# Writing three bfloat16 parts to DRAM once and repeating them in the loads of the stacks

## The chip, the cores and the metric

The kernel runs on one core of one Trainium2 chip. The metric is the device time of one execution in microseconds (us). The kernel before took 806.59 us in the median of three runs (804.44, 806.59 and 806.61).

## The reference

Two transformer layers with a layer norm behind each half run on x of 4 batches, 512 tokens and 256 features. Layer 0 has an attention with 16 query heads and 4 key heads of 16 features (RMS norm, rotary embedding, no mask) and a mixture of eight experts beside a shared one. Layer 1 has a causal attention with 16 query and 16 key heads and a feed-forward layer whose weights come in 4 bits with a low-rank addition. What the change touches is the product of queries and keys in both attentions:

```
logits = jnp.einsum('btkgh,bskh->bkgts', q * scale, k)          # layer 0
scores = jnp.einsum('bnqd,bnkd->bnqk', q, k) * scale            # layer 1
x = _layernorm(x + _L0_attn_ref(x, ...)); x = _layernorm(x + _L0_ffn_ref(x, ...))
x = _layernorm(x + _L1_attn_ref(x, ...)); x = _layernorm(x + _L1_ffn_ref(x, ...))
```

## The kernel before

**Stacks.** Everything is float32, but the scores are computed in bfloat16 and must be nearly as exact. Each of q and k is therefore split into three bfloat16 parts (part 0 is the rounded value, part 1 the rounded rest, part 2 the rest of that), and six products of parts are summed by one matmul: for each head a stack of 6 x 16 = 96 rows is made, where q holds its parts in the order 0,0,0,1,1,2 and k in the order 0,1,2,0,1,0. A matmul over the 96 rows then gives q0k0 + q0k1 + q0k2 + q1k0 + q1k1 + q2k0. The stacks are `q_stack` and `k_stack` in layer 0, `cq_stack` and `ck_stack` in layer 1, each with two buffers for alternate batches.

**The way of the parts.** The projections come out with features on partitions, ordered (feature, head), so that a head's 16 features don't lie together. The parts (`parts`, `cparts`: partitions x 3 x 512 tokens) go to DRAM and come back in stack order. `layer0_parts` (issued at L532) and the `cK` steps of SP's last loop (L643) write each part as many times as the stack has it, in three transfers: 3, 2 and 1 copies (for k: parts 0 to 2, parts 0 and 1, part 0). One store is 64 partitions (k of layer 0) or 128 partitions by 1 KB rows. Then `layer0_stacks` (L544 for k, L548 and L549 for the first eight heads of q, L553 for the last eight) and `layer1_stacks` (L628) load them. In layer 1 a load is a head group (four heads): 96 rows of 4 KB, one for q and one for k; two groups make a half (128 features), and a batch has two halves.

**Order of the work.** SP issues every one of these transfers from one queue in program order. In layer 0 it issues, for each batch: wait for the parts of k, store; wait for the parts of the first half of q, store; wait for the store of k, load k; wait for the store of q, load q in two transfers; wait for the parts of the second half, store, wait for that, load. Between the batches SP issues the loads of the expert weights (`gate_up_load`, L558; three of 1 MB after each of the first two batches, one after the third). In layer 1 each half is stored as its parts come (`cparts_ready`), and after the k of a half SP waits for the stores (`cs_scr`) and issues four loads. The second half of batch 1 comes behind step `cM` instead, at which SP also moves the row maxima into two more stack rows (`m_t`, two transfers at L650, semaphore `s_m`).

TensorE works through the lists `A_*` and `C_*` in their written order, and never goes ahead of a step that waits. `attS` (matmuls at L744) waits for `s_stack`, `s_stack1` or `s_stack2` at the first use of a load. In layer 1 `max` (L904, which finds the row maxima) is the first to use a stack and waits for `cs_stack` once per head group; `cattS` (L928) recomputes the scores with the maxima and waits for `s_m` at the start of a batch. ScalarE waits for the stores before it overwrites a part (`T` at L995, `cQ` at L1108).

Of the kernel before, what the change touches and what calls it, by code (L numbers as in the profile page):

```python
# [22 lines left out]
BF16 = mybir.dt.bfloat16  # L23
# [7 lines left out]
B = 4  # L31
# [119 lines left out]
def post_ln_layers(nc, ins, out):  # L151
# [4 lines left out]
    with ExitStack() as ctx:  # L156
# [193 lines left out]
        def cparts_of(b, i):  # L350

            return cparts_first[:, i % 2] if b == 0 and i >= 2 else cparts[:, i % 2]

        qscr = nc.dram_tensor("q_stacks_dram", [B, 2, 6, P, S], BF16).ap()
        kscr = nc.dram_tensor("k_stack_dram", [B, 6, KV0 * HD, S], BF16).ap()
        cscr = nc.dram_tensor("stacks_dram", [B, 2, 2, 6, P, S], BF16).ap()
# [148 lines left out]
        def _(sp):  # L505
# [17 lines left out]

            def layer0_parts(b, i):

                w = qk_width(i)
                for j in range(3):
                    if i == 0:
                        dst, src = kscr[b], parts[0:w, 0, 0:3 - j, :]
                    else:  # L530
                        dst, src = qscr[b, i - 1], parts[0:w, i % 2, j:j + 1, :].to_broadcast([w, 3 - j, S])
                    sp.dma_start(dst[(0, 3, 5)[j]:(3, 5, 6)[j]].rearrange("r p n -> p r n"), src).then_inc(s_scr[i % 2], 16)  # L532

            def layer0_stacks(b):

                sp.wait_ge(parts_ready, 3 * b + 1)
                layer0_parts(b, 0)
                sp.wait_ge(parts_ready, 3 * b + 2)
                layer0_parts(b, 1)
                sp.wait_ge(s_scr[0], 96 * b + 48)  # L540
                if b >= 2:

                    sp.wait_ge(pv_done, head0 * (b - 1))
                sp.dma_start(k_stack[0:STACK, b % 2, :, :], kscr[b].rearrange("r (d h) n -> (r d) h n", d=HD))\  # L544
# [7 lines left out]
                sp.wait_ge(s_scr[0], 96 * (b + 1))  # L552
                sp.dma_start(q_stack[0:STACK, b % 2, NH // 2:NH, :], qscr[b, 1].rearrange("r (d h) n -> (r d) h n", d=HD))\  # L553
                  .then_inc(s_stack2[b % 2], 16)
# [64 lines left out]
            def layer1_stacks(b, half):  # L619
                if b >= 2 and half == 0:  # L620

                    sp.wait_ge(pv_done, head0 * B + headc * (b - 1))
                for t in range(2):
                    sp.wait_ge(cs_scr[t][half], 48 * (b + 1))
                for hg in (2 * half, 2 * half + 1):
                    for t, dst in ((0, cq_stack), (1, ck_stack)):
                        rows = cscr[b, t, half].rearrange("r (d h) n -> (r d) h n", d=HD)
                        sp.dma_start(dst[0:STACK, b % 2, 4 * hg:4 * (hg + 1), :],  # L628
                                     rows[:, 4 * (hg % 2):4 * (hg % 2 + 1), :]).then_inc(cs_stack[hg][b % 2], 16)

            for step in c_steps:
                n, b, i = step
                if n == "cK":
                    half, of_k = i // 2, i % 2
                    sp.wait_ge(cparts_ready, 4 * b + i + 1)
                    for j in range(3):
                        if of_k:
                            dst = cscr[b, 1, half, (0, 3, 5)[j]:(3, 5, 6)[j]]
                            src = cparts_of(b, i)[:, 0:3 - j, :]
                        else:  # L640
# [21 lines left out]
        def _(pe):  # L662
# [48 lines left out]
            for step in a_steps:  # L711
# [20 lines left out]
                elif n == "attS":  # L732
                    hg, kt = i // NT, i % NT
                    if i == 0:
                        pe.wait_ge(s_stack[b % 2], 32 * (b // 2 + 1))
                    if hg == 1 and kt == 0:
                        pe.wait_ge(s_stack1[b % 2], 16 * (b // 2 + 1))
                    if hg == HG // 2 and kt == 0:
                        pe.wait_ge(s_stack2[b % 2], 16 * (b // 2 + 1))
# [110 lines left out]
            for step in c_steps:  # L850
# [45 lines left out]
                elif n == "max":  # L896

                    qt, h0, nh = MAXES[i]
                    if i % (len(MAXES) // HG) == 0:
                        pe.wait_ge(cs_stack[h0 // 4][b % 2], 32 * (b // 2 + 1))  # L900
# [68 lines left out]
        def _(act):  # L969
            copy = ACT.Copy  # L970
            for step in a_steps:
# [17 lines left out]
                elif n == "T":  # L989

                    if 3 * b + i >= 2:
                        act.wait_ge(s_scr[i % 2], 96 * b if i == 0 else 48 * b if i == 1 else 96 * b + 48)
# [69 lines left out]
            for step in c_steps:  # L1062
# [32 lines left out]
                elif n == "cQ":  # L1095
# [6 lines left out]
                    if b and i >= 2:  # L1102
                        act.wait_ge(cs_scr[i % 2][0], 48 * (b + 1))
                    elif b:
                        act.wait_ge(cs_scr[i % 2][0 if b == 1 else 1], 48 * b)
# [582 lines left out]
```

## Time and profile before

| | us |
|---|---|
| median of three runs | 806.59 |
| the profiled execution's own time | 804.52 |
| its span in the trace | 802.8 |
| TensorE (PE) busy | 755.4, 94% |
| VectorE (DVE) busy | 446.9, 56% |
| ScalarE (ACT) busy | 398.7, 50% |
| DMA queue of SP (q1) | 69.26 MB, 28.0% of the 16 engines' span |

A busy share is the time of an engine's instructions over the span. The trace names for each instruction its line (L744), its engine and what it waited for; a queue of an engine has a q behind its name (SPq). A transfer's packets are its contiguous rows and, beside them, the 4-byte packets by which the engines report completion. "Share of 16 engines" is the packets' time summed over a window and divided by 16 times the window. PEclk is the granted clock of TensorE as a share of 2.4 GHz, so 0.50 is 1.2 GHz.

### The profile page before, as it was taken

Reading aid. Unit: us, or ns where it says so; the run is one execution under the profiler, and the core shown is the slowest. Engines: PE = TensorE matmul, PEld = TensorE weight load, DVE = VectorE, ACT = ScalarE, POOL = GpSimd, SP = SyncE. Lnnn points to the kernel's source line nnn. Section 1 sums busy time; section 2 is a strip of 40 time slices with the busy share of each in tenths; the row PEclk is TensorE's granted clock in tenths of the full one; section 3 lists DMA queues with packets and bytes.
Section 4 is the critical chain, followed back from the end, with each engine's and each line's share of the span. In section 5 each row is a group of like instructions: output and inputs, shape, how many; then the busy total and the mean of one; then the engine's idle time right before and its main releaser. Section 6 shows DMA issues by size and latency. Waiting matters only on the chain. (4 is left out here: it accounts for less than half of the span.)

```text
span 802.8 us, 12486 instructions
## 1 busy us (share of the span) xinstructions
PE 755.4 (94%) x4393; PEld 446.3 (56%) x4394; DVE 446.9 (56%) x1194; ACT 398.7 (50%) x593; POOL 126.8 (16%) x135
## 2 busy tenths in 40 slices
PE   8899999999999999999999897989989998999996
PEld 4323434444434589999977554435445644653685
DVE  4663744565354722222228798939685667563464
ACT  3499775786595154454525325465333453146230
POOL 0000000000000131111563372223101110022100
PEclk9999999999999999999999999989999999999999
DMA  7668116105106262111123882005600280000000
GB/s 230 182 204 280 43 35 191 51 27 155 42 27 218 72 183 76 46 52 46 39 70 109 242 260 81 2 2 153 189 1 3 79 234 6 26 1 27 0 27 27
DMA packets 53822, 75.03 MB, mean 93 GB/s; under 512 B 7926, under 2 KB 45082, under 8 KB 53386
## 3 DMA queue, kind: packets, MB, share of 16 engines
q1 hardware_dynamic: 51900, 69.26, 28.0%
q0 software_dynamic: 1872, 5.11, 2.4%
q8 instruction: 30, 0.49, 0.3%
q14 instruction: 20, 0.16, 0.1%
HBM read 46.57 MB, written 27.66 MB: 92 GB/s over the span
## 5 line engine op out<-in xcount | busy, mean ns | idle before, releaser
L676 PE MATMUL ps<-arena 128*128 128x256 f32 (+3 forms) x1084 | 315.8, 439 | 5.6 <-DVE arena L1217 1.4
L676 PEld LDWEIGHTS ps<-arena 128*128 128x128 f32 x1084 | 196.1, 190 | 87.9 <-issue 55.4
L1003 ACT ACTIVATE arena<-ps 128x1024 f32<-128x1024 f32 x128 | 124.1, 1029 | 25.6 <-PE ps L744 25.3
L1118 ACT ACTIVATE arena<-ps 128x1024 f32<-128x1024 f32 (+3 forms) x128 | 82.9, 702 | 99.0 <-PE ps L928 98.8
L1496 DVE TENSOR_REDUCE arena<-ps 128x1 f32<-128x384 f32 (+3 forms) x176 | 100.5, 634 | 26.0 <-PE ps L906 25.3
L806 PE MATMUL ps<-arena 128*128 128x128 f32 x736 | 89.4, 275 | 0.6 <-DVE arena L1228 0.6
L806 PEld LDWEIGHTS ps<-arena 128*128 128x128 f32 x736 | 87.4, 192 | 2.4 <-issue 1.3
L1622 POOL TENSOR_SCALAR_AFFINE_SELECT arena<-arena 128x512 f32<-128x512 f32 x64 | 42.5, 664 | 218.4 <-ACT arena L1118 218.4
L904 PE MATMUL ps<-arena 96*128 96x128 bf16 (+3 forms) x256 | 62.3, 306 | 12.0 <-DVE arena L1496 7.3
L744 PE MATMUL ps<-arena 96*128 96x512 bf16 x256 | 69.7, 382 | 4.2 <-ACT arena L1003 2.7
L758 PE MATMUL ps<-arena 128*32 128x512 f32 x512 | 68.8, 604 | 0.3 <-ACT arena L1010 0.3
L744 PEld LDWEIGHTS ps<-arena 96*128 96x128 bf16 x256 | 17.8, 97 | 77.5 <-ACT arena L1003 40.7
L928 PE MATMUL ps<-arena 98*128 98x512 bf16 (+3 forms) x256 | 47.8, 307 | 4.9 <-ACT arena L1118 2.7
L941 PE MATMUL ps<-arena 128*32 128x128 f32 (+3 forms) x512 | 49.0, 454 | 2.8 <-POOL arena L1622 1.8
L906 PE MATMUL ps<-arena 128*128 128x128 bf16 x256 | 49.5, 223 | 0.0
L904 PEld LDWEIGHTS ps<-arena 96*128 96x128 bf16 x256 | 25.3, 99 | 39.0 <-DVE arena L1496 19.6
L928 PEld LDWEIGHTS ps<-arena 98*128 98x128 bf16 x256 | 18.2, 98 | 47.6 <-issue 31.4
L1541 POOL TENSOR_TENSOR arena<-arena 128x1024 f32<-128x1024 f32 x1 | 1.9, 1895 | 265.7 <-DVE arena L1326 265.7
L815 PE MATMUL ps<-arena 128*128 x184 | 43.4, 379 | 0.0
L1031 ACT ACTIVATE arena<-ps 128x512 f32<-128x512 f32 x23 | 13.7, 597 | 55.8 <-PE ps L806 55.8
L668 PE MATMUL ps<-arena 128*128 128x128 f32 (+3 forms) x237 | 33.9, 280 | 7.7 <-DVE arena L1270 3.2
L668 PEld LDWEIGHTS ps<-arena 128*128 128x128 f32 (+3 forms) x237 | 28.1, 141 | 20.5 <-issue 8.6
(160 smaller groups left out, 755.3 us busy)
## 6 DMA issues: line engine op xcount, KB each, us to landing
arena<-stacks_dram SPq DMA_DIRECT2D x32, 384.0 KB, 6.3
arena<-in_gate_up_proj SPq DMA_DIRECT2D x8, 1024.0 KB, 9.3
stacks_dram<-arena SPq DMA_DIRECT2D x16, 384.0 KB, 3.7
arena<-in_down_proj SPq DMA_DIRECT2D x8, 512.0 KB, 9.0
stacks_dram<-arena SPq DMA_DIRECT2D x16, 256.0 KB, 4.0
q_stacks_dram<-arena SPq DMA_DIRECT2D x8, 384.0 KB, 3.3
arena<-q_stacks_dram SPq DMA_DIRECT2D x8, 384.0 KB, 4.8
arena<-q_stacks_dram SPq DMA_DIRECT2D x4, 768.0 KB, 5.8
```

Of the source, the lines that this page charges most:

```text
L668: last = nc.tensor.transpose(dst[0:rows, col:col + n], src, idn)
L676: last = nc.tensor.matmul(dst[0:rows, lo:hi], a, w, start=(n == 0), stop=(n == len(pairs) - 1))
L744: last = nc.tensor.matmul(ps[:, g, :], k_stack[0:STACK, b % 2, hg, cols(kt)], q_stack[0:STACK, b % 2, 4 * hg + g, :], start=True, stop=True)
L758: last = nc.tensor.matmul(ps[32 * g:32 * g + 32, 4, :], v_aug[:, kt, hg, :], (probs0, probs1)[i % 2][:, g, :], start=(kt == 0), stop=(kt = ...
L806: last = nc.tensor.matmul(ps[:, 2 * half + up, cols(f)], of_expert[:, up, c, cols(f)], xg_t[:, half, c, :], start=(c == 0), stop=(c == 1))
L904: nc.tensor.matmul(dst[:, w * g:w * (g + 1)], cq_stack[0:STACK, b % 2, h0 + g, cols(qt)], ck_stack[0:STACK, b % 2, h0 + g, 0:w], start=Tru ...
L906: last = nc.tensor.matmul(dst[:, w * g + P * qt:w * (g + 1)], identb, negmask, start=False, stop=True, skip_group_check=True)
L928: last = nc.tensor.matmul(ps[:, g, P * kt:S], ck_stack[0:STACK + 2, b % 2, h, cols(kt)], cq_stack[0:STACK + 2, b % 2, h, P * kt:S], start= ...
L941: last = nc.tensor.matmul(ps[32 * g:32 * g + 32, 4, P * kt:S], cv_aug[:, b % 2, kt, 4 * hg + g, :], cprobs[:, i % 2, g, P * kt:S], start=( ...
L1003: nc.scalar.activation(probs[:, 2 * p:2 * p + 2, :], ps[:, 2 * p:2 * p + 2, :], ACT.Exp)\
L1118: nc.scalar.activation(cprobs[:, i % 2, 2 * p:2 * p + 2, P * kt:S], ps[:, 2 * p:2 * p + 2, P * kt:S], ACT.Exp).then_inc(exp_done[p], 1)
L1496: nc.vector.tensor_reduce(mneg[:, qt, h0:h0 + nh], filled(v, step)[:, 0:nh * w].rearrange("p (h n) -> p h n", n=w), AX.X, ALU.max, negate= ...
```

## The change

The DRAM tensors shrink from six to three parts. `store_parts` writes each part once: k with one transfer, q with two (parts 0 and 1 to places 1 and 2, part 2 to place 0). `load_stack` makes the six copies: q with two transfers (parts 0 and 1 repeated twice as the first 64 rows by a source dimension of size 2 and stride 0, then parts 2 and 0 as the last 32 rows), k with three (part 0 twice as 32 rows, part 1 twice as 32 rows, parts 0 and 2 as 32 rows). The order of the six products in a stack is another, their sum the same. The waits count the new numbers of transfers.

```diff
-        qscr = nc.dram_tensor("q_stacks_dram", [B, 2, 6, P, S], BF16).ap()
-        kscr = nc.dram_tensor("k_stack_dram", [B, 6, KV0 * HD, S], BF16).ap()
-        cscr = nc.dram_tensor("stacks_dram", [B, 2, 2, 6, P, S], BF16).ap()
+        qscr = nc.dram_tensor("q_parts_dram", [B, 2, 3, P, S], BF16).ap()
+        kscr = nc.dram_tensor("k_parts_dram", [B, 3, KV0 * HD, S], BF16).ap()
+        cscr = nc.dram_tensor("parts_dram", [B, 2, 2, 3, P, S], BF16).ap()
...
+            def store_parts(dst, parts_of, of_k, done):
+
+                if of_k:
+                    sp.dma_start(dst.rearrange("r p n -> p r n"), parts_of).then_inc(done, 16)
+                else:
+                    sp.dma_start(dst[1:3].rearrange("r p n -> p r n"), parts_of[:, 0:2, :]).then_inc(done, 16)
+                    sp.dma_start(dst[0:1].rearrange("r p n -> p r n"), parts_of[:, 2:3, :]).then_inc(done, 16)
+
+            def load_stack(dst, src, heads, of_k, done):
+
+                if of_k:
+                    for r in range(2):
+                        one = src[r].rearrange("(d h) n -> d h n", d=HD)[:, heads, :]
+                        sp.dma_start(dst[2 * HD * r:2 * HD * (r + 1)], one.unsqueeze(0).to_broadcast([2] + list(one.shape)))\
+                          .then_inc(done, 16)
+                    last = src[0:3:2].rearrange("r (d h) n -> r d h n", d=HD)[:, :, heads, :]
+                else:
+                    low = src[1:3].rearrange("r (d h) n -> (r d) h n", d=HD)[:, heads, :]
+                    sp.dma_start(dst[0:4 * HD], low.unsqueeze(0).to_broadcast([2] + list(low.shape))).then_inc(done, 16)
+                    last = src[0:2].rearrange("r (d h) n -> (r d) h n", d=HD)[:, heads, :]
+                sp.dma_start(dst[4 * HD:6 * HD], last).then_inc(done, 16)
...
-                sp.wait_ge(s_scr[0], 96 * b + 48)
+                sp.wait_ge(s_scr[0], 48 * b + 16)
...
-                sp.dma_start(k_stack[0:STACK, b % 2, :, :], kscr[b].rearrange("r (d h) n -> (r d) h n", d=HD))\
-                  .then_inc(s_stack[b % 2], 16)
-                sp.wait_ge(s_scr[1], 48 * (b + 1))
-                rows = qscr[b, 0].rearrange("r (d h) n -> (r d) h n", d=HD)
-                sp.dma_start(q_stack[0:STACK, b % 2, 0:4, :], rows[:, 0:4, :]).then_inc(s_stack[b % 2], 16)
-                sp.dma_start(q_stack[0:STACK, b % 2, 4:8, :], rows[:, 4:8, :]).then_inc(s_stack1[b % 2], 16)
+                load_stack(k_stack[0:STACK, b % 2, :, :], kscr[b], slice(0, KV0), True, s_stack[b % 2])
+                sp.wait_ge(s_scr[1], 32 * (b + 1))
+                load_stack(q_stack[0:STACK, b % 2, 0:4, :], qscr[b, 0], slice(0, 4), False, s_stack[b % 2])
+                load_stack(q_stack[0:STACK, b % 2, 4:8, :], qscr[b, 0], slice(4, 8), False, s_stack1[b % 2])
...
+                load_stack(q_stack[0:STACK, b % 2, NH // 2:NH, :], qscr[b, 1], slice(0, 8), False, s_stack2[b % 2])
...
                 for hg in (2 * half, 2 * half + 1):
                     for t, dst in ((0, cq_stack), (1, ck_stack)):
-                        rows = cscr[b, t, half].rearrange("r (d h) n -> (r d) h n", d=HD)
-                        sp.dma_start(dst[0:STACK, b % 2, 4 * hg:4 * (hg + 1), :],
-                                     rows[:, 4 * (hg % 2):4 * (hg % 2 + 1), :]).then_inc(cs_stack[hg][b % 2], 16)
+                        load_stack(dst[0:STACK, b % 2, 4 * hg:4 * (hg + 1), :], cscr[b, t, half],
+                                   slice(4 * (hg % 2), 4 * (hg % 2 + 1)), t == 1, cs_stack[hg][b % 2])
...
-                    for j in range(3):
-                        if of_k:
-                            dst = cscr[b, 1, half, (0, 3, 5)[j]:(3, 5, 6)[j]]
-                            src = cparts_of(b, i)[:, 0:3 - j, :]
-                        else:
-                            dst = cscr[b, 0, half, (0, 3, 5)[j]:(3, 5, 6)[j]]
-                            src = cparts_of(b, i)[:, j:j + 1, :].to_broadcast([P, 3 - j, S])
-                        sp.dma_start(dst.rearrange("r p n -> p r n"), src).then_inc(cs_scr[of_k][half], 16)
+                    store_parts(cscr[b, of_k, half], cparts_of(b, i), of_k, cs_scr[of_k][half])
...
-                        pe.wait_ge(s_stack[b % 2], 32 * (b // 2 + 1))
+                        pe.wait_ge(s_stack[b % 2], 80 * (b // 2 + 1))
```

## Rows read from the trace of the kernel before

**Rows 1.** The profile's page: the span and TensorE's busy time.
```profile
span 802.8 us, 12486 instructions
...
PE 755.4 (94%) x4393; PEld 446.3 (56%) x4394; DVE 446.9 (56%) x1194; ACT 398.7 (50%) x593; POOL 126.8 (16%) x135
```

**Rows 2.** Waits of PE: who waited for whom, us in total, times, longest.
```profile
PE ps L904 <- DMA arena<-stacks_dram: 0.5, 1, 0.5
```

**Rows 3.** DMA issues on the page: count, KB each, median us to landing.
```profile
arena<-stacks_dram SPq DMA_DIRECT2D x32, 384.0 KB, 6.3
...
arena<-arena SPq DMA_DIRECT2D x8, 16.0 KB, 2.1
```

**Rows 4.** DMA view, 417.63 to 419.9 us; queue rows: packets, MB, share.
```profile
DMA packets 113, 0.32 MB, mean 141 GB/s; under 512 B 37, under 2 KB 53, under 8 KB 111
...
q1 hardware_dynamic: 27, 0.08, 12.7%
```

**Rows 5.** DMA view, 418.9 to 420.5 us: SP's queue.
```profile
q1 hardware_dynamic: 2, 0.00, 0.2%
```

**Rows 6.** DMA view, 700 to 720 us: SP's queue.
```profile
DMA packets 65, 0.04 MB, mean 2 GB/s; under 512 B 32, under 2 KB 64, under 8 KB 64
...
q1 hardware_dynamic: 64, 0.03, 0.7%
```

**Rows 7.** Windows: length, busy time (x instructions) of each engine, PEclk, DMA share, GB/s.
```profile
76.00:82.00 6.00, 6.00 (x35) 2.75 (x34) 2.58 (x5) 3.93 (x9) 0.00 (x0) 1.00 1.03 409
485.00:492.00 7.00, 5.60 (x41) 2.57 (x39) 6.52 (x27) 4.62 (x6) 3.02 (x3) 1.00 0.83 225
```

**Rows 8.** Timeline of SP, layer 0: start, time to issue, line, transfers.
```profile
27.57 0.62 SPq L544 DMA_DIRECT2D arena<-k_stack_dram  x1
...
37.48 1.98 SPq L558 DMA_DIRECT2D arena<-in_gate_up_proj  x3
...
124.66 0.60 SPq L544 DMA_DIRECT2D arena<-k_stack_dram  x1
```

**Rows 9.** Timeline of PE, layer 0: first scores of batches 0, 1, 2.
```profile
34.88 1.03 PE L744 MATMUL ps<-arena 96*128 96x512 bf16 x4
...
71.81 1.34 PE L744 MATMUL ps<-arena 96*128 96x512 bf16 x4
...
136.16 1.04 PE L744 MATMUL ps<-arena 96*128 96x512 bf16 x4
```

**Rows 10.** Timeline of SP, layer 1: stores and loads of batch 0, loads of batch 2.
```profile
437.72 3.86 SPq L643 DMA_DIRECT2D stacks_dram<-arena  x6
443.77 1.73 SPq L628 DMA_DIRECT2D arena<-stacks_dram  x4
...
557.01 1.73 SPq L628 DMA_DIRECT2D arena<-stacks_dram  x4
```

**Rows 11.** Timeline of PE, layer 1: first use of each stack, in batches 0 and 2.
```profile
452.87 0.31 PE L904 MATMUL ps<-arena 96*128 96x128 bf16 x1
...
461.46 0.22 PE L904 MATMUL ps<-arena 96*128 96x128 bf16 x1
...
467.19 0.22 PE L904 MATMUL ps<-arena 96*128 96x128 bf16 x1 [0.24 <-DVE arena L1496]
...
474.86 0.22 PE L904 MATMUL ps<-arena 96*128 96x128 bf16 x1
...
486.19 0.60 PE L928 MATMUL ps<-arena 98*128 98x512 bf16 x2 [0.30 <-DMA arena<-arena]
...
563.03 0.23 PE L904 MATMUL ps<-arena 96*128 96x128 bf16 x1 [0.48 <-DMA arena<-stacks_dram]
...
585.86 0.22 PE L904 MATMUL ps<-arena 96*128 96x128 bf16 x1
```

**Rows 12.** Windows around the start of layer 1 (columns as in rows 7).
```profile
449.40:452.90 3.50, 1.61 (x14) 1.30 (x13) 2.92 (x4) 1.62 (x4) 2.58 (x2) 0.99 1.02 326
452.90:456.30 3.40, 3.40 (x21) 2.53 (x19) 2.24 (x4) 0.60 (x1) 0.00 (x0) 0.50 0.77 268
```

**Rows 13.** Windows: the stretch of layer 1's attention (columns as in rows 7).
```profile
430.00:695.00 265.00, 241.37 (x1486) 128.88 (x1485) 198.89 (x443) 110.50 (x174) 63.36 (x77) 0.98 0.34 102
```

**Rows 14.** Waits of ACT for stores of parts.
```profile
ACT arena L1108 <- DMA stacks_dram<-arena: 6.8, 2, 5.0
...
ACT arena L995 <- DMA k_stack_dram<-arena: 6.6, 2, 3.3
```

More of the change, by code:

```diff
@@ L522, in _ @@
             sp.dma_start(s_down, ins["shared_down_w"].rearrange("(c p) n -> p c n", p=P)).then_inc(s_w1, 16)
+            def store_parts(dst, parts_of, of_k, done):
[16 more added lines that the diff above has]
+                sp.dma_start(dst[4 * HD:6 * HD], last).then_inc(done, 16)
             def layer0_parts(b, i):
                 w = qk_width(i)
-                for j in range(3):
-                    if i == 0:
-                        dst, src = kscr[b], parts[0:w, 0, 0:3 - j, :]
-                    else:
-                        dst, src = qscr[b, i - 1], parts[0:w, i % 2, j:j + 1, :].to_broadcast([w, 3 - j, S])
-                    sp.dma_start(dst[(0, 3, 5)[j]:(3, 5, 6)[j]].rearrange("r p n -> p r n"), src).then_inc(s_scr[i % 2], 16)
+                store_parts(qscr[b, i - 1] if i else kscr[b], parts[0:w, i % 2], i == 0, s_scr[i % 2])
             def layer0_stacks(b):
@@ L623, in layer1_stacks @@
                 for t in range(2):
-                    sp.wait_ge(cs_scr[t][half], 48 * (b + 1))
+                    sp.wait_ge(cs_scr[t][half], (32, 16)[t] * (b + 1))
                 for hg in (2 * half, 2 * half + 1):
                     for t, dst in ((0, cq_stack), (1, ck_stack)):
-                        rows = cscr[b, t, half].rearrange("r (d h) n -> (r d) h n", d=HD)
-                        sp.dma_start(dst[0:STACK, b % 2, 4 * hg:4 * (hg + 1), :],
-                                     rows[:, 4 * (hg % 2):4 * (hg % 2 + 1), :]).then_inc(cs_stack[hg][b % 2], 16)
+                        load_stack(dst[0:STACK, b % 2, 4 * hg:4 * (hg + 1), :], cscr[b, t, half],
+                                   slice(4 * (hg % 2), 4 * (hg % 2 + 1)), t == 1, cs_stack[hg][b % 2])
             for step in c_steps:
@@ L734, in _ @@
                     if i == 0:
[L735 removed]
+                        pe.wait_ge(s_stack[b % 2], 80 * (b // 2 + 1))
                     if hg == 1 and kt == 0:
[L737 removed]
+                        pe.wait_ge(s_stack1[b % 2], 32 * (b // 2 + 1))
                     if hg == HG // 2 and kt == 0:
[L739 removed]
+                        pe.wait_ge(s_stack2[b % 2], 32 * (b // 2 + 1))
                     for g in range(4):
@@ L899, in _ @@
                     if i % (len(MAXES) // HG) == 0:
-                        pe.wait_ge(cs_stack[h0 // 4][b % 2], 32 * (b // 2 + 1))
+                        pe.wait_ge(cs_stack[h0 // 4][b % 2], 80 * (b // 2 + 1))
                     dst = take(pe, step)
@@ L991, in _ @@
                     if 3 * b + i >= 2:
-                        act.wait_ge(s_scr[i % 2], 96 * b if i == 0 else 48 * b if i == 1 else 96 * b + 48)
+                        act.wait_ge(s_scr[i % 2], 48 * b if i == 0 else 32 * b if i == 1 else 48 * b + 16)
                     src = filled(act, step)
@@ L1102, in _ @@
                     if b and i >= 2:
-                        act.wait_ge(cs_scr[i % 2][0], 48 * (b + 1))
+                        act.wait_ge(cs_scr[i % 2][0], (32, 16)[i % 2] * (b + 1))
                     elif b:
-                        act.wait_ge(cs_scr[i % 2][0 if b == 1 else 1], 48 * b)
+                        act.wait_ge(cs_scr[i % 2][0 if b == 1 else 1], (32, 16)[i % 2] * b)
                     for dst in (qf[i % 2], cparts_of(b, i)[:, 0, :]):
```

6 lines of the change are left out of this document (1 added, 5 removed).

## The prediction

> **What bounds the kernel now.** I read the page first: TensorE is busy in 94% of a span of 802.8 us [rows 1], so a change can gain at most the few per cent in which it idles, and loses whatever it makes TensorE wait. Then the waits of PE: the stacks' loads held it for 0.5 us in all [rows 2]. The transfers are thus hidden today, and the question is whether they stay hidden. For that I set SP's timeline beside PE's [rows 8 to 11]: a load of a stack is issued 6 to 12 us ahead of its first use, and lands in 6.3 us [rows 3]. There is little to spare.
>
> **How many engines a load gets.** This decides the sum. A transfer's 4-byte completions show how many of the 16 engines carry it. The two transfers of the row maxima (16 rows of 1 KB each) gave 32 data packets and 32 completions, so 16 engines each [rows 6]. The load at L617 has two rows of 32 KB: two packets of over 8 KB (113 less 111) [rows 4], and then two completions [rows 5], so two engines, though 64 KB would have fed all. The count follows the outermost rows, not the bytes. In the changed loads the source's outermost dimension is the repeat (or, for k's last load, the pair of parts 0 and 2, which lie apart), of size 2, while the destination still counts 64 or 32 partitions. No row shows such a mixed case. If the destination alone decided, all 16 engines would work and the sum would be about nothing; if an engine needs an even share of both sides, it is two engines. I take two: an engine that does whole outermost rows of the source cannot have less than one of them, and rows 4 and 5 are the only ones with a size of 2.
>
> The Trainium skill, "DMA: Bandwidth & Descriptors", section "Why a DMA increments its semaphore by 16 and not by 1", says that the engine count is the largest number up to 16 that divides the outermost sizes of both sides, and that a DMA from SP takes the lowest-numbered engines. By that rule the mixed case goes on two engines and the sum is the one below; the trace agrees where both sides are 2 [rows 4, 5], and no run here shows the mixed case. Its "Rules for kernel authors" name "a leading zero-stride broadcast of c copies" as confined to c engines.
>
> **The price of a row.** With 4 KB rows all engines at work moved 409 GB/s at a share of 1.03 in the loads of expert weights, 24.8 bytes per ns and engine, 0.165 us a row; in the loads of stacks 225 GB/s at 0.83, 16.9 bytes per ns, 0.24 us [rows 7]. The two engines of L617 ran beside a gather: 12.7% of 16 engines in 2.27 us is 4.6 us for 0.08 MB, 17 bytes per ns [rows 4]. I take 0.165, because two engines alone move some 50 GB/s and load neither DRAM nor SBUF as the 16 do; 0.24 is the other bound. From issue to landing a small transfer takes 2.1 us [rows 3].
>
> **The change part by part.** (1) Stores: half the bytes, and 3 transfers for 6 in a half of layer 1. What they free is at most ScalarE's waits for them, 13.4 us in four [rows 14]; PE works beside these, so I count nothing, 13.4 us being the other bound. (2) Issue: a half costs SP now 3.86 + 1.73 us for 6 stores and 4 loads [rows 10]; with 3 and 10 it is 1.9 + 4.3, 0.6 us more, beside the 27 us below. (3) The loads on two engines. A head group of layer 1 has for each of the two 32 rows of q, 48 of k (three transfers), and 2 of q's 16-engine load: 82 rows, 13.5 us, where 16 engines had 12 rows each. In layer 0, k and the first group of q make the same 82 rows, the second group 34, the last eight heads as much as 68.
>
> Layer 0 [rows 8, 9]. Batch 0: 27.57 + 2.1 + 13.5 = 43.2, used at 34.88: 8.3 us late. Batch 1: the pair is at work on 116 rows until 46.7; the store of the third part queues behind them on the same engines and lands 2.1 later, then 11.2 for its load, 7.9 for three expert loads queued next (48 rows), and 2.1 until batch 1's stores, behind all this, land: 70. Its loads land at 70 + 15.6 = 85.6, where they are used at 71.81 + 8.3 = 80.1: 5.5 more. Batch 2: 124.66 + 15.6 = 140.3 for 136.16, 4.1, and batch 3 the same. Sum 22 us.
>
> Layer 1 [rows 10, 11]; the lateness is carried along. Batch 0, group 0: 443.77 + 15.6 = 459.4 for 452.87, 6.5 late; group 1: 472.9 for 461.46, 11.4 late. The stores of the second half stand behind these loads: landed at 475, loads at 490.6 for 467.19, 23.4 late; group 3 at 504.1 for 474.86, 29.2 late. SP has then queued the first half of batch 1, 2.1 + 2.1 + 27 us, to 535.3, and the row maxima behind it, one row on each engine; `cattS` needs them at 486.19: 49.1 late. Batch 1's own groups were loaded meanwhile. Batch 2 starts afresh: 557.01 + 15.6 = 572.6 for 563.03, 9.6 late; its second half 572.6 + 13.5 + 2.1 + 15.6 = 603.8 for 585.86, 17.9 late. Batch 3 the same. Sum 49.1 + 2 x 17.9 = 85 us.
>
> (4) The clock. After a stretch in which PE was busy 1.61 of 3.50 us, the granted clock was 0.50 (1.2 GHz) for the next 3.40 us [rows 12], which gives away 1.7 us of full speed. The waits above of over 3 us are 4 in layer 0, 5 in batch 0 of layer 1, 2 in each of its batches 2 and 3: 13, so 22 us (nothing, if those stretches are not bound by PE).
>
> The sum is 22 + 85 + 22 = 129 us on the profiled execution's 804.5: 933.5. The median of the runs lies 2.1 above that execution, so **936**. With 0.24 us a row the same steps give 59 us in layer 0 and 179 in layer 1, and 19 waits of over 3 us cost 32: 1077. At the other end leave out the clock's 22 us and the 20 us that the queued row maxima add in batch 0, and let later work take back the 24 us in which PE idles in layer 1's attention (265.00 less 241.37) [rows 13]: 63 us, 870.
>
> **The rivals.**
> (a) *All 16 engines.* The destination's partitions decide, and the change only moves bytes: loads as before, the first use of batches 2 and 3, which already waits 0.48 us [rows 11], 0.6 us later each for the issue; layer 0 about 1 us sooner. 807, no change. For it: the destination has 64 or 32 rows, and each earlier load used 16 engines for such counts. Against: rows 4 and 5.
> (b) *Faster, on 16 engines.* The same count of engines, and the halved stores release ScalarE's buffers: of its 13.4 us of waits [rows 14] half reach PE. 800. This decides where a store's landing stands in PE's chain; against it speaks that PE hardly waits for ScalarE there. It also needs (a)'s condition.
> (c) *A pair of its own for each load.* Two engines each, but different ones, so that the loads of a group run beside each other: 5.6 us for q's rows instead of 13.5 for all. Batch 0 of layer 0: 27.57 + 2.1 + 5.6 + 1.3 for three more issues = 36.6, 1.7 late; batch 0 of layer 1 in time; batch 2 and 3: 557.01 + 2.1 + 5.6 + 0.4, 2.1 late each. 6 us, 813. Nothing in the rows tells which engines L617 had.
>
> **How the numbers follow.** A measurement of this kernel can tell about 0.3%, 2.4 us. The forecast has 0.84: its one unproven step is that the size of 2 decides though the other side has 64, and the rows have no case against it. (c) has 0.04, also slower; (a) 0.07; (b) 0.05. Slower therefore 0.88, the same 0.07, faster 0.05. The range is the main case's own, 870 to 1080: its low end the 63 us, its high end the dearer row; it leaves out (a), (b), (c) and a small tail of the main case.
>
> **What would show it.** In the changed profile the loads of stacks should land in 7 to 15 us and more instead of 6.3, with SP's queue at a DMA share near 2/16 for tens of us; the count of completions should fall, since most of the loads give 2 instead of 16; PE should wait for `DMA arena<-parts_dram` at L904, for the row maxima at L928 in batch 0, and for `q_parts_dram` and `k_parts_dram` at L744, some 100 us in all; more slices of PEclk should be under 9. I am wrong if the loads still land in about 6 us (then (a) or (b)); if each lands in 7 us with several at once, it is (c); if the share is near 2/16 but PE's waits are under 60 us, the order of the queue hides more than I found.

## The result, and the profile after

The changed kernel takes 934.86 us in the median of three runs (933.64 to 936.9) where the kernel before takes 806.59: a ratio of 1.159, 95% interval 1.1556 to 1.1623. The forecast was 936. Its profiled execution took 936.9 us beside a span of 935.2, so the difference to explain is 935.2 less 802.8 [rows 1], 132.4 us.

The profile's page of the changed kernel, its first lines, the queue of SP, and one line of the DMA issues (count, KB each, median us to landing):

```profile
span 935.2 us, 12514 instructions
...
PE 790.5 (85%) x4393; PEld 462.5 (49%) x4394; DVE 446.8 (48%) x1194; ACT 399.5 (43%) x593; POOL 126.5 (14%) x135
...
PEclk9788899899899999999997676999779988899998
...
q1 hardware_dynamic: 41132, 59.03, 19.3%
...
parts_dram<-arena SPq DMA_DIRECT2D x8, 384.0 KB, 12.2
```

Read the PE line against [rows 1] first. TensorE has the same 4393 instructions, and is busy 35.1 us more (790.5 for 755.4): its mean granted clock was 0.919 of full speed, where it was 0.99 before. Its idle time, span less busy, rose from 47.4 to 144.7, by 97.3. Together that is the 132.4. Then the queue: it moves 59.03 MB where it moved 69.26, so the change did save the bytes that it was meant to save; and yet time was lost.

The waits of PE, changed kernel (who waited for whom, us in total, times, longest; L910 answers to L904 of [rows 2], L750 to L744, L934 to L928):

```profile
PE ps L910 <- DMA arena<-parts_dram: 51.1, 7, 10.5
PE ps L750 <- DMA arena<-q_parts_dram: 30.6, 6, 9.1
PE ps L934 <- DMA arena<-arena: 16.1, 2, 14.3
PE ps L682 <- ACT arena L1114: 8.0, 1, 8.0
```

The row maxima cost TensorE something before as well; the line of the kernel before is

```profile
PE ps L928 <- DMA arena<-arena: 2.1, 2, 1.8
```

So where loads of stacks [rows 2] and row maxima held TensorE for 0.5 + 2.1 = 2.6 us, they now hold it for 97.8, and the fourth line is a load's delay too, that comes through ScalarE. The same view of ACT shows it waiting behind a store:

```profile
ACT arena L1114 <- DMA parts_dram<-arena: 35.1, 2, 34.7
```

ScalarE must not overwrite a part until its store has landed. The store stands behind loads on two slow engines, ScalarE waits 34.7 us for it, and TensorE in the end 8.0 for ScalarE. [Rows 14] had 6.8 us of this in all.

That two engines do the work is seen directly. The DMA view of the changed kernel from 505 to 515 us, 40 slices of 0.25 us (busy share in tenths, and GB/s):

```profile
DMA  9998111111111111111111111111111111111111
GB/s 385 373 381 291 74 49 49 49 49 66 49 49 49 49 66 49 49 49 49 66 49 49 49 49 66 49 49 49 49 66 49 49 49 41 53 57 41 45 49 49
```

In the first slices a store on all 16 engines passes. From then on the share is 1 to 2 tenths, and the rate is 49 GB/s in four slices and 66 in the fifth, though SP had by then queued all five loads of this head group. Five such slices are 16 rows of 4 KB in 1.25 us: 52.4 GB/s, 26.2 bytes per ns for each of two engines, 0.156 us for a row on one of them; the forecast had taken 0.165 [rows 7]. Several loads were open at once and the share stays near 2/16, so they all share one pair.

The Trainium skill, "DMA: Bandwidth & Descriptors", section "Why a DMA increments its semaphore by 16 and not by 1", has the engine count from the outermost sizes of both sides and the engines from the lowest number up. The trace agrees on the count, now also for the mixed case of 2 on one side and 32 or 64 on the other: two engines, and the same two for all loads open in this window. Which numbers the two have, it does not show.

PE's timeline, changed kernel, the waits as they come (start, us, line, tile, and in brackets the idle time before and what ended it):

```profile
43.91 0.61 PE L750 MATMUL ps<-arena 96*128 96x512 bf16 x1 [9.15 <-DMA arena<-q_parts_dram]
...
70.71 0.61 PE L750 MATMUL ps<-arena 96*128 96x512 bf16 x1 [5.83 <-DMA arena<-q_parts_dram]
...
502.00 0.29 PE L910 MATMUL ps<-arena 96*128 96x128 bf16 x1 [6.27 <-DMA arena<-parts_dram]
...
514.80 0.29 PE L910 MATMUL ps<-arena 96*128 96x128 bf16 x1 [3.27 <-DMA arena<-parts_dram]
...
533.41 0.29 PE L910 MATMUL ps<-arena 96*128 96x128 bf16 x1 [10.49 <-DMA arena<-parts_dram]
...
548.67 0.76 PE L682 MATMUL ps<-arena 128*128 128x256 f32 x1 [7.99 <-ACT arena L1114]
...
579.66 0.61 PE L934 MATMUL ps<-arena 98*128 98x512 bf16 x1 [14.31 <-DMA arena<-arena]
```

The first three of layer 1 are the first uses of [rows 11] at 452.87, 461.46 and 467.19, here 49.1, 53.3 and 66.2 us late. From 502.00 to 514.80 one head group is served: 12.8 us, which is 82 rows at 0.156, where the forecast had 13.5.

SP's timeline, changed kernel, around batch 0 of layer 1 (start, us to issue, line, transfers; L537 is k's first two loads, L542 q's first):

```profile
486.02 1.30 SPq L537 DMA_DIRECT2D arena<-parts_dram  x2
...
489.02 7.11 SPq L537 DMA_DIRECT2D arena<-parts_dram  x2
496.17 2.69 SPq L544 DMA_DIRECT2D arena<-parts_dram  x1
498.90 2.42 SPq L529 DMA_DIRECT2D parts_dram<-arena  x1
...
516.76 0.52 SPq L542 DMA_DIRECT2D arena<-parts_dram  x1
...
548.17 0.52 SPq L542 DMA_DIRECT2D arena<-parts_dram  x1
...
579.32 0.56 SPq L542 DMA_DIRECT2D arena<-parts_dram  x1
```

The same line took 1.30 us for its two loads and then, 3 us later, 7.11: issuing itself is held up, and every transfer behind it starts later. It happens where the pair's work has piled up; that this is the reason is likely, and was not tested by itself. The stores of the second half are issued at 498.90 and after, and the loads that wait for them only at 516.76.

### The profile page after: what moved, and what is told of

It is laid out like the page before. It is cut to its first block and busy times, and to the rows that moved or that the text cites. A ratio compares the mean times of both kernels' runs of the same rounds, so it can differ in the third digit from the quotient of the medians.

```text
span 935.2 us, 12514 instructions
## 1 busy us (share of the span) xinstructions
PE 790.5 (85%) x4393; PEld 462.5 (49%) x4394; DVE 446.8 (48%) x1194; ACT 399.5 (43%) x593; POOL 126.5 (14%) x135
## 3 DMA queue, kind: packets, MB, share of 16 engines
q1 hardware_dynamic: 41132, 59.03, 19.3%
## 5 line engine op out<-in xcount | busy, mean ns | idle before, releaser
L682 PE MATMUL ps<-arena 128*128 128x256 f32 (+3 forms) x1084 | 327.0, 451 | 13.4 <-ACT arena L1114 8.0
L682 PEld LDWEIGHTS ps<-arena 128*128 128x128 f32 x1084 | 203.3, 197 | 100.5 <-issue 68.1
L910 PE MATMUL ps<-arena 96*128 96x128 bf16 (+3 forms) x256 | 70.3, 340 | 59.2 <-DMA arena<-parts_dram 51.1
L750 PE MATMUL ps<-arena 96*128 96x512 bf16 x256 | 76.5, 416 | 32.9 <-DMA arena<-q_parts_dram 30.6
L812 PEld LDWEIGHTS ps<-arena 128*128 128x128 f32 x736 | 87.4, 192 | 2.4 <-issue 1.3
L750 PEld LDWEIGHTS ps<-arena 96*128 96x128 bf16 x256 | 19.2, 102 | 111.8 <-issue 35.9
L910 PEld LDWEIGHTS ps<-arena 96*128 96x128 bf16 x256 | 28.6, 112 | 89.2 <-DMA arena<-parts_dram 55.9
L764 PE MATMUL ps<-arena 128*32 128x512 f32 x512 | 72.0, 630 | 0.0
L934 PE MATMUL ps<-arena 98*128 98x512 bf16 (+3 forms) x256 | 51.2, 322 | 18.9 <-DMA arena<-arena 16.1
L912 PE MATMUL ps<-arena 128*128 128x128 bf16 x256 | 56.9, 247 | 0.0
L934 PEld LDWEIGHTS ps<-arena 98*128 98x128 bf16 x256 | 18.7, 100 | 64.8 <-issue 35.3
L1114 ACT ACTIVATE arena<-ps,arena 128x512 f32<-128x512 f32 (+1 forms) x32 | 20.1, 684 | 63.9 <-DMA parts_dram<-arena 35.1
## 6 DMA issues: line engine op xcount, KB each, us to landing
arena<-in_gate_up_proj SPq DMA_DIRECT2D x8, 1024.0 KB, 11.3
parts_dram<-arena SPq DMA_DIRECT2D x8, 384.0 KB, 12.2
```

Of the source, the lines that this page charges most:

```text
L682: last = nc.tensor.matmul(dst[0:rows, lo:hi], a, w, start=(n == 0), stop=(n == len(pairs) - 1))
L750: last = nc.tensor.matmul(ps[:, g, :], k_stack[0:STACK, b % 2, hg, cols(kt)], q_stack[0:STACK, b % 2, 4 * hg + g, :], start=True, stop=True)
L764: last = nc.tensor.matmul(ps[32 * g:32 * g + 32, 4, :], v_aug[:, kt, hg, :], (probs0, probs1)[i % 2][:, g, :], start=(kt == 0), stop=(kt = ...
L812: last = nc.tensor.matmul(ps[:, 2 * half + up, cols(f)], of_expert[:, up, c, cols(f)], xg_t[:, half, c, :], start=(c == 0), stop=(c == 1))
L910: nc.tensor.matmul(dst[:, w * g:w * (g + 1)], cq_stack[0:STACK, b % 2, h0 + g, cols(qt)], ck_stack[0:STACK, b % 2, h0 + g, 0:w], start=Tru ...
L912: last = nc.tensor.matmul(dst[:, w * g + P * qt:w * (g + 1)], identb, negmask, start=False, stop=True, skip_group_check=True)
```

## The experiments

The theory: two engines carry every load whose source has an outermost size of 2, all on one pair; the waits and the lower clock behind them make the whole difference. Against it stood that zero stride itself is slow, that the halved stores or the greater number of transfers matter, and that one queue's order, not the pair's work, sets the time.

**1. The repeat as an inner dimension.** The same number of loads, the same bytes; the size of 2 stands second in the source, behind the features, and k's parts are loaded feature by feature.

```diff
-                    for r in range(2):
-                        one = src[r].rearrange("(d h) n -> d h n", d=HD)[:, heads, :]
-                        sp.dma_start(dst[2 * HD * r:2 * HD * (r + 1)], one.unsqueeze(0).to_broadcast([2] + list(one.shape)))\
-                          .then_inc(done, 16)
-                    last = src[0:3:2].rearrange("r (d h) n -> r d h n", d=HD)[:, :, heads, :]
+                    pair = src[0:2].rearrange("r (d h) n -> d r h n", d=HD)[:, :, heads, :]
+                    for r in range(2):
+                        sp.dma_start(dst[2 * HD * r:2 * HD * (r + 1)], pair).then_inc(done, 16)
+                    last = src[0:3:2].rearrange("r (d h) n -> d r h n", d=HD)[:, :, heads, :]
...
-                    sp.dma_start(dst[0:4 * HD], low.unsqueeze(0).to_broadcast([2] + list(low.shape))).then_inc(done, 16)
-                    last = src[0:2].rearrange("r (d h) n -> (r d) h n", d=HD)[:, heads, :]
+                    sp.dma_start(dst[0:4 * HD], low.unsqueeze(1).to_broadcast([2 * HD, 2] + list(low.shape[1:]))).then_inc(done, 16)
+                    last = src[0:2].rearrange("r (d h) n -> d r h n", d=HD)[:, :, heads, :]
```

> Same stores, same number of loads and the same bytes as the changed kernel, but the repeat of q is the inner of the source's two row dimensions, and k is loaded feature by feature with the parts inside, so that every source counts 16 or 32 rows on the outside. Theory (the outermost size of the source sets the number of engines): 16 engines again, no waits for stacks, 800 to 810 us, against 934.9. Rival (it is the repeated reading itself, or the larger number of transfers, that costs): above 900 us.

Measured: 803.92 us, ratio to the kernel before 0.9965 (0.9945 to 0.9985). The page of this kernel:

```profile
PE 756.1 (94%) x4393; PEld 445.7 (56%) x4394; DVE 446.5 (56%) x1194; ACT 398.6 (50%) x593; POOL 126.8 (16%) x135
...
q1 hardware_dynamic: 42364, 59.04, 23.9%
...
arena<-parts_dram SPq DMA_DIRECT2D x64, 128.0 KB, 3.4
...
parts_dram<-arena SPq DMA_DIRECT2D x8, 384.0 KB, 2.5
```

The bytes are those of the changed kernel (59.04 MB), the loads and stores as many; the completions rise by 1232 packets (42364 for 41132), since more engines report. The number says how many: the changed kernel has 88 loads with a 2 outermost (24 in layer 0, 64 in layer 1), and if each of them goes from 2 completions to 16, that is 88 x 14 = 1232, exactly. So each of these loads had two engines, whatever the other side's size. A load lands in 3.4 us, the store that took 12.2 in 2.5, and TensorE waits for no load of a stack. So neither zero stride nor the number of transfers costs anything that shows here: the place of the 2 in the access pattern is the whole 131 us. This version beats both kernels, the one before by 0.35% (0.15 to 0.55). Its view of ACT's waits shows one thing that got better:

```profile
ACT arena L1113 <- DMA parts_dram<-arena: 0.4, 1, 0.4
```

That was 6.8 us [rows 14]. Whether this is where the 0.35% comes from was not tried.

**2 and 3. One layer alone.** Layer 1 (then layer 0) gets the stores, loads and waits of the kernel before.

```diff
-        cscr = nc.dram_tensor("parts_dram", [B, 2, 2, 3, P, S], BF16).ap()
+        cscr = nc.dram_tensor("stacks_dram", [B, 2, 2, 6, P, S], BF16).ap()
...
-                        load_stack(dst[0:STACK, b % 2, 4 * hg:4 * (hg + 1), :], cscr[b, t, half],
-                                   slice(4 * (hg % 2), 4 * (hg % 2 + 1)), t == 1, cs_stack[hg][b % 2])
+                        rows = cscr[b, t, half].rearrange("r (d h) n -> (r d) h n", d=HD)
+                        sp.dma_start(dst[0:STACK, b % 2, 4 * hg:4 * (hg + 1), :],
+                                     rows[:, 4 * (hg % 2):4 * (hg % 2 + 1), :]).then_inc(cs_stack[hg][b % 2], 16)
```

> The change in layer 0 alone. The changed kernel is 42.8 us behind the one before at the last score group of layer 0, so the theory (each layer pays for its own waits) says 806.6 + 43 = 850 us, 844 to 855. Rival (the cost of layer 1 grows out of a queue that layer 0 leaves behind): less or more than this, and the two single layers don't add up to the whole.

> The change in layer 1 alone. From the last group of layer 0 on, the changed kernel falls back by another 89.6 us: theory 896 us, 890 to 902, and with the run of layer 0 alone the two sum to 128 us within 6. Rival as there.

Measured: layer 0 alone 848.07 us, ratio 1.051 (1.0477 to 1.0543), 42.5 us more than the median of before; layer 1 alone 894.18, ratio 1.1094 (1.1063 to 1.1126), 88.7 more. Waits of PE of the first, then of the second:

```profile
PE ps L758 <- DMA arena<-q_parts_dram: 30.9, 5, 8.6
```

```profile
PE ps L918 <- DMA arena<-parts_dram: 51.4, 8, 11.1
PE ps L942 <- DMA arena<-arena: 16.5, 2, 14.6
```

These are the waits of the full change, layer by layer, and 42.5 + 88.7 = 131.2 is its 128.3 nearly: the layers do not help each other.

**4. The old order of rows.** The stacks keep the order 0,0,0,1,1,2 of before: k in plain loads of 48, 32 and 16 rows, q in repeats of 3 and 2 and one plain load.

```diff
+                for lo, hi, r, n in (((0, 48, 0, 3), (48, 80, 0, 2), (80, 96, 0, 1)) if of_k else
+                                     ((0, 48, 1, 0), (48, 80, 2, 0), (80, 96, 0, 1))):
+                    if n:
+                        one = src[r:r + n].rearrange("r (d h) n -> (r d) h n", d=HD)[:, heads, :]
+                    else:
+                        one = src[r].rearrange("(d h) n -> d h n", d=HD)[:, heads, :]
+                        one = one.unsqueeze(0).to_broadcast([(hi - lo) // HD] + list(one.shape))
+                    sp.dma_start(dst[lo:hi], one).then_inc(done, 16)
```

> Parts stored once as in the change, but the order of rows of the kernel before: k needs no repeat (three loads of 48, 32 and 16 plain rows), q repeats part 0 three times and part 1 twice, with the repeat outside. By the theory q's loads go on three and two engines, and the two busiest engines have 39 rows a head group instead of 82, 6.2 us instead of 13: most of it is then covered by the 6 to 12 us that the loads are issued ahead, 9 to 11 us of waits and two or three drops of the clock, 815 to 825 us. Rival (the cost is in proportion to the rows on the busiest engines): 39/82 of 128 us, 868 us. If all of q's repeat counted for nothing: 806 us.

Measured: 847.58 us, ratio 1.0526 (1.0488 to 1.0564): both missed, and the truth lies between them. Waits of PE of this kernel, then SP's queue on its page and in the DMA view from 474 to 482 us (packets, MB, share), then SP's timeline:

```profile
PE ps L907 <- DMA arena<-parts_dram: 17.3, 4, 6.8
PE ps L747 <- DMA arena<-q_parts_dram: 7.6, 2, 5.5
```

```profile
q1 hardware_dynamic: 42056, 59.04, 25.0%
```

```profile
q1 hardware_dynamic: 296, 0.89, 65.2%
```

```profile
453.70 6.58 SPq L541 DMA_DIRECT2D arena<-parts_dram  x12
...
473.95 6.67 SPq L541 DMA_DIRECT2D arena<-parts_dram  x12
...
494.57 6.54 SPq L541 DMA_DIRECT2D arena<-parts_dram  x12
```

The counts of engines are as the theory has them. A stack of q has loads with 3, 2 and 16 outermost, 3 + 2 + 16 = 21 completions, where run 1 has two loads on 16 engines, 32; 28 stacks of q make 28 x 11 = 308 fewer, and 42364 less 42056 is 308.

The price of a row is not. The halves follow each other every 20.3 and 20.6 us. With 39 rows a group on the busiest engines, two groups at 0.165 and 2.1 for the stores would make 15.0; 20.4 less 2.1 over 78 rows is 0.23 us a row. By the same count the changed kernel, whose loads start at 516.76, 548.17 and, for the next half, 579.32, has 0.18 (31.3 less 2.1 over 164 rows). Both counts hold the stores' own share of the pair and the time until the first load starts, so they lie above the 0.156 of the pair alone. In the window the 16 engines are busy 65.2% of 8 us for 0.89 MB, 10.7 bytes per ns and engine, for 26.2 where the pair works alone: where confined loads (those on two or three engines) run among loads on all engines, everything is dearer. The direction of the theory holds (39 rows cost 42 us where 82 cost 128).

**5. The row maxima out of SP's queue.** ScalarE issues the two transfers that stood behind the loads of batch 1.

```diff
-                    for j in range(2):
-                        sp.dma_start(cq_stack[STACK + j:STACK + j + 1, b % 2, :, :], m_t[NH * j:NH * (j + 1), :])\
-                          .then_inc(s_m, 16)
...
+                    consumed(act, step)
+                    for j in range(2):
+                        nc.scalar.dma_start(cq_stack[STACK + j:STACK + j + 1, b % 2, :, :], m_t[NH * j:NH * (j + 1), :])\
+                          .then_inc(s_m, 16)
```

> The changed kernel with the two transfers of the row maxima issued by ScalarE, on its own queue, so that they don't stand behind the loads of batch 1. PE waited 14.3 us for them in batch 0 of layer 1. Theory (the two engines are the bound of this stretch, the queue only decides what waits for them): that wait goes to under 4 us, but batch 1's second half, whose loads start after these transfers as before, then comes late for its own use, and most is given back: 928 to 934 us. Rival (the place in the queue is what costs): the full 12 us, 923 us or less.

Measured: 936.02 us, ratio 1.1602 (1.1564 to 1.164): no gain over 934.86, and 2 us above the theory's range. PE's timeline of this kernel says why:

```profile
568.38 0.39 PE L931 MATMUL ps<-arena 98*128 98x512 bf16 x1 [3.19 <-DMA arena<-arena]
...
597.64 0.29 PE L907 MATMUL ps<-arena 96*128 96x128 bf16 x1 [7.64 <-DMA arena<-parts_dram]
...
610.44 0.29 PE L907 MATMUL ps<-arena 96*128 96x128 bf16 x1 [2.21 <-DMA arena<-parts_dram]
```

The wait of 14.31 us shrinks to 3.19, and 7.64 and 2.21 appear later, at the second half of batch 1, which had been hidden behind it. The queue's order decides where TensorE waits; what the pair has to carry decides how much.

**6. k's last rows as two plain loads.** The load of parts 0 and 2, which has an outermost 2 but no zero stride, becomes two loads of 16 rows.

```diff
-                    last = src[0:3:2].rearrange("r (d h) n -> r d h n", d=HD)[:, :, heads, :]
+                    for r in (0, 2):
+                        one = src[r].rearrange("(d h) n -> d h n", d=HD)[:, heads, :]
+                        sp.dma_start(dst[4 * HD + HD * r // 2:5 * HD + HD * r // 2], one).then_inc(done, 16)
```

> The changed kernel with k's last 32 rows (parts 0 and 2, no repeat, outermost size 2) loaded as two plain transfers of 16 rows. Theory (it is the size of 2, repeat or not): these 16 rows an engine leave the pair, 68 instead of 82 rows a group, 10.9 instead of 13.1 us; the prediction's steps then give 64 us of waits instead of 100, with the clock some 85: 880 to 900 us. Rival (only a stride of zero confines a load): no change, 932 to 937.

Measured: 904.36 us, ratio 1.1223 (1.1167 to 1.1279), 30.5 less than the full change. PE's timeline, first two groups of layer 1, and SP's queue on the page:

```profile
488.00 0.29 PE L912 MATMUL ps<-arena 96*128 96x128 bf16 x1 [5.30 <-DMA arena<-parts_dram]
...
498.61 0.23 PE L912 MATMUL ps<-arena 96*128 96x128 bf16 x1 [1.79 <-DMA arena<-parts_dram]
```

```profile
q1 hardware_dynamic: 41732, 59.03, 20.4%
```

A group now takes 10.6 us, for 12.8, with 16 rows less on each of the two engines and 2 more from the plain loads: 14 rows at 0.156 are 2.2. The packets are 600 more than in the changed kernel (41732 for 41132): 20 stacks of k, each with two loads of 16 completions for one of 2. An outermost 2 over parts that lie apart is thus confined as a zero stride is, and the rival falls. By size the gain stayed just short of what was expected.

**7. Useless matmuls ahead of the waits of layer 1.** They are meant to keep TensorE busy up to the wait, so that its clock is full behind it.

```diff
+            FILLS = {(0, 0): 23, (0, 2): 42, (2, 0): 36, (2, 2): 28, (3, 0): 30, (3, 2): 25, (0, "m"): 58}
...
+                for _ in range(n):
+                    nc.tensor.matmul(dst, identb, negmask.unsqueeze(1).to_broadcast([P, NT, P]), start=True, stop=True)
```

> The changed kernel with matmuls of no use (their result is overwritten) ahead of seven of layer 1's waits, of 5 to 13 us each and shorter than the wait by about 1 us, so that the clock stays up. PE's busy time grew by 19 us in layer 1. If all of it cost time: 916 us. By the lateness at the first uses only batches 2 and 3 lost time beyond their waits, 3 and 5 us, since in batch 0 the next wait takes in what the clock loses: theory 926 to 929 us. If the clock costs nothing: 935.

Measured: 933.48 us, ratio 1.1593 (1.1546 to 1.164): no gain beyond the interval. A window of the changed kernel, then two of this one (columns as in [rows 7]):

```profile
514.80:530.00 15.20, 8.10 (x36) 4.43 (x36) 6.31 (x11) 0.00 (x0) 0.89 (x1) 0.72 0.16 54
```

```profile
520.00:536.00 16.00, 14.60 (x77) 7.40 (x78) 5.15 (x9) 0.00 (x0) 0.00 (x0) 1.00 0.24 90
...
664.00:676.00 12.00, 10.10 (x45) 4.99 (x46) 3.98 (x7) 2.70 (x4) 0.64 (x1) 0.72 0.29 109
```

In batch 0 the clock is at 1.00 from 520 to 536 us, where the changed kernel had 0.72; it still fell to 0.74 between 500 and 520 and to 0.66 between 536 and 556, so the run takes away a part of the clock's loss. Of that part nothing is won: from the end of layer 0's attention to batch 1 of `cattS` the lateness against the kernel before grows by 52.5 us (39.4 to 91.9), where it grew by 50.4 in the changed kernel (42.8 to 93.2). In batch 2 the clock fell as well (0.72), so there the run tells nothing.

**8 and 9. The same in layer 0.** Calls of `keep_clock`, two matmuls of 128 x 512 each, ahead of the waits of layer 0; those of batch 0 of layer 1 go. Run 8 has 19, 11, 7, 9 and 13 calls; at 0.87 us a call these outlast the waits (16.5 us for the first, against 9.1). Run 9 has 9, 6, 3, 4 and 6.

```diff
+            FILLS = {(2, 0): 46, (2, 2): 26, (3, 0): 36, (3, 2): 34}
+            FILLS0 = {(0, 0): 9, (0, 2): 6, (1, 0): 3, (2, 0): 4, (3, 0): 6}
...
+                    if kt == 0 and (b, hg) in FILLS0:
+                        if head0 * b + i:
+                            pe.wait_ge(exp_done[0], head0 * b + i)
+                        keep_clock(FILLS0[b, hg])
```

> The changed kernel with useless matmuls ahead of five waits of layer 0 (3 to 8 us each) and of four in batches 2 and 3 of layer 1, better fitted to the waits than in the run before. In the changed kernel the lateness grows by 2.3 to 3.5 us in the group behind each of layer 0's waits (13.6 us in all) and by 1.4 to 2.8 behind those of batches 2 and 3 (8.9 us). Theory (that growth is the lower clock after a wait): it goes, 913 to 920 us. Rival (it is not the clock; or the waits take in what the clock gives back): 929 to 936 us.

> As the run with useless matmuls in layer 0 before it, with about half as many, fitted to the waits (9, 6, 3, 4 and 6 calls at 0.87 us against measured waits of 9.1, 5.8, 3.7, 4.7 and 6.5 us); those of batches 2 and 3 of layer 1 stay. Theory (behind a wait TensorE runs at the lower clock for a while, and that is what makes the lateness grow in layer 0): the growth of 13.6 us in layer 0 goes and 2 to 3 us in layer 1 with it; 934.9 less 13 to 17 makes 918 to 922. Rival (the time is set by the transfers there too, and the clock's loss is taken back later): 930 to 936.

Measured: run 8 943.08 us, ratio 1.1675 (1.164 to 1.1711); run 9 930.54, ratio 1.1543 (1.1512 to 1.1574). Both missed, and 9 ends on the rival's side. Windows of layer 0, changed kernel, then run 8 (PEclk is the third figure from the right):

```profile
34.00:56.00 22.00, 12.59 (x47) 2.55 (x45) 10.06 (x31) 9.60 (x19) 0.00 (x0) 0.69 0.35 112
...
71.00:96.00 25.00, 20.87 (x110) 5.89 (x109) 7.02 (x13) 17.93 (x21) 0.00 (x0) 0.84 0.24 82
```

```profile
34.00:56.00 22.00, 21.00 (x63) 8.57 (x61) 10.07 (x31) 5.72 (x15) 0.00 (x0) 1.00 0.39 132
...
71.00:96.00 25.00, 24.41 (x122) 8.00 (x124) 7.03 (x13) 16.20 (x20) 0.00 (x0) 1.00 0.20 69
```

The lateness of `attS` in layer 0 (start of the first matmul on each stack or group, less that in the kernel before, us):

| batch, group | 0,0 | 0,1 | 0,2 | 0,3 | 1,0 | 1,1 | 1,3 | 2,0 | 2,3 | 3,0 | 3,3 |
|---|---|---|---|---|---|---|---|---|---|---|---|
| changed kernel | 9.0 | 11.3 | 17.2 | 19.9 | 23.6 | 25.9 | 25.8 | 30.6 | 33.4 | 39.3 | 42.8 |
| run 9 | 8.3 | 7.7 | 15.7 | 18.4 | 22.7 | 22.7 | 25.8 | 30.6 | 30.6 | 36.1 | 38.5 |

In the changed kernel the lateness grows in the group behind each of the five waits while nothing is waited for, by 2.3 to 2.8 us, 12.8 in all (9.0 to 11.3, 30.6 to 33.4; in batch 3 the last 0.7 us before 42.8 are a wait of 0.74). With the clock at 1.00 it does not: in run 8 it stands at 24.9, 31.0, 38.8 and 49.3 through whole groups and batches, in run 9 at 30.6 through batch 2. So this growth is the clock's work. Run 9 took away four of the five, 10.1 us, and yet was only 4.3 us less late at the end of layer 0; its median is 4.3 lower, not the 13 to 17 expected. Behind the second wait, where 2.62 us of it were left, the clock still fell (0.87 from 69 to 82 us). PE's timeline at the first scores of batch 2, run 9:

```profile
166.79 1.04 PE L762 MATMUL ps<-arena 96*128 96x512 bf16 x4 [1.29 <-DMA arena<-q_parts_dram]
```

The changed kernel starts these at 166.79 as well, after a wait of 4.71; there the useless matmuls fill what was a wait, and the load comes when it comes. What batches 0 and 1 had saved is gone by then: the table's rows meet at 25.8, through a wait of 1.39 us at 121.80 that the changed kernel does not have, and a lower clock at another place (0.85 from 122 to 145). What batches 2 and 3 saved was kept in the main. How much of the 4.3 us is the clock at all is open: the two intervals overlap (1.1556 to 1.1623 and 1.1512 to 1.1574), and run 7, whose layer 0 is that of the changed kernel, ended that layer at 39.4 in its profiled execution, as near to run 9's 38.5 as to the 42.8.

## Why the prediction was right, and where it was not

**How many engines a load gets: right.** This one unproven step carried 0.84 of the chance. The share of 2/16 shows it, the counts of completions in runs 1, 4 and 6 confirm it to the packet, and runs 1 and 6 show that the outermost size decides, zero stride or not. Rival (a) is out (TensorE waits 97.8 us for what it left at 2.6), (b) with it; (c) is out since the open loads of a group run at two engines' rate in all. (b) lives on in run 1, at 804, where loads no longer hold TensorE; what makes those 0.35% was not tried.

**The price of a row: near enough for this kernel** (0.156 us for 0.165, a group 12.8 for 13.5), because two engines run alone for most of the time. Run 4 shows where it would have been wrong. The range's high end is not sound: with 0.24 us a row the printed steps come to at most 170 us in layer 1 instead of 179, so that 1077 is some 10 us too high; nothing measured turns on it.

**The sum: right by two errors that cancel.** That 936 lies 1.1 us from the 934.86 measured is luck: layer 0 cost 13.8 us more than forecast, layer 1 10.4 less. Waits are from PE's timeline (layer 0 is 9.1 + 5.8 + 3.7 + 4.7 + 6.5 + 0.7, the 30.6 of L750), the clock is the remainder that the lateness has beyond them:

| us | forecast | measured |
|---|---|---|
| layer 0, waits | 22 | 30.6 |
| layer 0, clock (4 waits of 1.7) | 7 | 12.2 |
| layer 1, waits | 85 | 73.4 |
| layer 1, clock (9 waits of 1.7) | 15 | 16.2 |
| sum | 129 | 132.4 |

Runs 2 and 3 say the same with times: 42.5 for layer 0, forecast 29; 88.7 for layer 1, forecast 100.

In *step (3), layer 0* what failed is the load of batch 0's last eight heads. By the step's own figures it lands at 46.7 + 2.1 + 11.2 = 60.0, for a use at 53.48 in the kernel before and 8.3 later here, so no wait was counted; it held TensorE until 70.71, for 5.8 us. SP's timeline of the changed kernel:

```profile
30.09 3.51 SPq L544 DMA_DIRECT2D arena<-q_parts_dram  x1
...
50.18 0.49 SPq L542 DMA_DIRECT2D arena<-q_parts_dram  x1
...
51.19 1.45 SPq L572 DMA_DIRECT2D arena<-in_gate_up_proj  x3
```

The load is issued at 50.18, where the step had 48.8, so that SP was held up ahead of it (3.51 us for one load at 30.09) is the smaller part. From there to its use it took some 20.5 us for 11.2, with three loads of expert weights issued 1 us behind it for all engines; how much of the 9 us is theirs was not taken apart. Batches 2 and 3 waited 4.7 and 6.5 for 4.1 each; batch 1 waited 3.7 for 5.5.

In *step (3), layer 1* the waits of batches 2 and 3 were 9.2 + 7.4 and 7.6 + 6.8 for 9.6 + 8.3 each, and the row maxima cost 14.3 for 19.9. That they stand behind the loads of batch 1 was right, but not as a price of its own: run 5 takes them out of the queue and gains nothing. The low end of the range counted on 20 us there, and could not have come about in that way. The 5.8 us of the second half's last group came as 8.0, and by another path than the step had: through ScalarE, held by a store that stood behind the loads.

In *step (1)* the stores were counted at nothing. They became slower, 12.2 us to land, where the same store lands in 2.5 when the loads have all 16 engines (run 1), for a part of each store must pass the pair behind the loads: in the DMA view above the bulk of the second half's stores is through by 506, and SP could issue the loads that wait for them only at 516.76.

In *step (2)* the ten loads of a half took SP 13.9 us to issue in the first half (from 484.98) for 4.3. That stays beside the pair's 27 us, as the step had it.

In *step (4)* the size was of the right order (28.4 us as a remainder, 35.1 by TensorE's busy time, for 22), but a sum that adds it to the waits is not quite what happens. TensorE does lose that time. Where the useless matmuls took a part of the loss away, the medians fell by 1.4 us (run 7) and 4.3 (run 9): in batch 0 of layer 1 nothing came back, and of 10.1 us in layer 0 4.3 were left, since at the next wait the load often comes no sooner than before. So the 22 us do not wholly stand beside the waits; without them some waits would have been longer. What is left when the whole loss is removed was not shown, as no run kept the clock up throughout.

## What to carry to other kernels

Before a DMA is counted as hidden, look at the outermost size of both its sides: if one is 2, two engines carry it (with 3 it was three, run 4), and all such transfers queue on the same two; put the repeat, or the index of parts, inside and a dimension of 16, 32 or 64 outside, as run 1 did, and the same transfer is hidden again. Where a slow queue feeds the bottleneck engine, a better order of the queue or a faster engine may gain little: here runs 5, 7 and 9 came to 936.02, 933.48 and 930.54 for 934.86, because most of what was taken from one wait went into others. Check a sum that comes out right by its parts, as two runs of one layer each did here.

## What was not expected of the hardware

- Issuing can itself be held up: two loads took SP 7.11 us at 489.02 and 1.30 at 486.02, where the pair's work had piled up. In run 1, where loads land in 3.4 us, they take 1.23.
- One confined load slows the ordinary ones behind it: a store of 384 KB landed in 12.2 us instead of 2.5.
- A row of 4 KB cost 0.156 us where two engines worked alone. Counted over whole halves, stores included, it was 0.18 us there and some 0.23 with confined and ordinary loads mixed (run 4, worked out above).
